# A two-layer graph network on one core: weight columns turned to rows on VectorE instead of TensorE, and the last pair of graphs done graph by graph

## The reference

```python
# layer 0: one attention weight per node, softmax over the 128 nodes of a graph
q, k = split(x @ Wqk);  v = x @ Wv
agg = adj @ (k * mask)
w = mask * sum(q * agg, axis=-1) / 16          # 128 numbers per graph
x = layernorm(x + softmax(w) * v)
# layer 1: edge weights adj * exp(q k^T), rows scaled to one
query, key, value = x @ Wq.T + bq, x @ Wk.T + bk, x @ Wv1.T + bv
weight = adj * exp(query @ key.T)
x = layernorm(x + (weight / weight.sum(-1)) @ value)
```

## Time and profile before

| | |
|---|---|
| median of 3 runs | 293.14 us (292.75 to 293.14) |
| the profiled execution | 292.77 us, of it the span of the trace 291.0 us |
| PE busy | 283.4 us, 97% of the span |
| DVE busy | 253.9 us, 87% |
| ACT busy | 238.2 us, 82% |
| POOL busy | 217.4 us, 75% |
| share of PE in the chain that ended last | 96% |
| granted clock of TensorE, mean | 0.997 |

### The profile page before, as it was taken

How to read it: one execution, slowest core, us unless ns; L and a number is a source line. 1 busy time by engine, 2 the same in 40 slices (tenths; PEclk the granted TensorE clock), 3 DMA queues, 4 the chain that set the end, 5 groups by cost and what they waited for, 6 DMA issues and landing times.

```text
span 291.0 us, 7075 instructions
## 1 busy us (share of the span) xinstructions
PE 283.4 (97%) x1984; PEld 263.7 (91%) x1984; DVE 253.9 (87%) x783; ACT 238.2 (82%) x568; POOL 217.4 (75%) x269
## 2 busy tenths in 40 slices
PE   8999999999999999999999999999999999999991
PEld 7789999999999999999999999999999999999980
DVE  1478999999989999999998999899999999999784
ACT  3455779899888989988898998889899888987862
POOL 1556987778898778789887788987787898877331
PEclk9999999999999999999999999999999999999998
DMA  7931323333334423334433333444233344210112
GB/s 241 332 97 37 91 93 127 93 91 98 106 125 126 126 93 88 99 100 126 126 124 95 88 99 100 126 126 126 94 87 96 103 126 126 90 57 26 46 38 108
DMA packets 19165, 31.26 MB, mean 107 GB/s; under 512 B 2128, under 2 KB 6608, under 8 KB 19152
## 3 DMA queue, kind: packets, MB, share of 16 engines
q1 hardware_dynamic: 19152, 31.11, 34.7%
HBM read 22.71 MB, written 8.39 MB: 107 GB/s over the span
## 4 chain that ended last, share of the span: by engine, by line
PE 96%; issue 1%; DVE 1%; POOL 0%; POOLq 0%; ACT 0%; DVEq 0%
PE ps L890 25%; PE ps L891 25%; PE ps L892 25%; PE ps L993 9%; PE ps L973 5%; PE ps L941 1%; PE ps L1112 1%; PE ps L913 1%; PE ps L1117 1%; PE ps L998 1%; PE ps L1126 1%; DVE x L661 0%; PE ps L952 0%; PE ps L960 0%; POOLq L42 0%
## 5 line engine op out<-in xcount | busy, mean ns | idle before, releaser
L890 PE MATMUL ps<-w_hi,xt_hi 128*128 128x512 f32 x124 | 49.3, 398 | 0.0
L891 PE MATMUL ps<-w_lo,xt_hi 128*128 128x512 f32 x124 | 48.6, 392 | 0.0
L892 PE MATMUL ps<-w_hi,xt_lo 128*128 128x512 f32 x124 | 48.3, 390 | 0.0
L372 POOL TENSOR_TENSOR edge_lo<-edge,edge_hi 128x256 fp32r<-128x256 f32 x29 | 21.6, 743 | 34.5 <-ACT edge_hi L544 34.5
L461 ACT ACTIVATE x<-x_sum,shift,rstd 128x256 f32<-128x256 f32 x60 | 32.8, 595 | 15.3 <-POOL shift L386 15.3
L305 POOL TENSOR_TENSOR x1b<-x,bv_all 128x512 f32<-128x512 f32 x31 | 39.7, 1282 | 2.9 <-DVE x L823 2.0
L359 POOL TENSOR_TENSOR xt_lo<-xt_raw,xt_hi 128x512 fp32r<-128x512 f32 x31 | 40.1, 1294 | 1.8 <-ACT xt_hi L443 1.8
L383 POOL TENSOR_TENSOR rstd<-var_eps,minus_half 128x4 f32<-128x4 f32 x31 | 31.6, 1018 | 9.0 <-DVE var_eps L799 9.0
L890 PE MATMUL ps<-x1t_hi,at_hi 128*128 128x256 f32 x124 | 37.4, 302 | 0.0
L366 POOL TENSOR_TENSOR x_lo<-x_raw,x_hi 128x512 fp32r<-128x512 f32 x28 | 36.2, 1294 | 0.0
L890 PE MATMUL ps<-wv_hi,x1t_hi 128*128 128x258 f32 x124 | 35.5, 286 | 0.0
(11 more groups left out here) (166 smaller groups left out, 909.5 us busy)
## 6 DMA issues: line engine op xcount, KB each, us to landing
xt_raw<-xt_pairs SPq DMA_DIRECT2D x32, 256.0 KB, 2.7
x_raw<-x_pairs SPq DMA_DIRECT2D x32, 256.0 KB, 2.7
out_pairs<-x SPq DMA_DIRECT2D x31, 256.0 KB, 2.0
adjt<-adjt_pairs SPq DMA_DIRECT2D x32, 129.0 KB, 2.1
p<-params SPq DMA_DIRECT2D x1, 770.0 KB, 6.7
p<-params SPq DMA_DIRECT2D x1, 512.0 KB, 3.8
p<-params SPq DMA_DIRECT2D x1, 256.0 KB, 4.6
out_pairs<-x SPq DMA_DIRECT2D x2, 128.0 KB, 1.8
```

What stands on the lines that cost most here:

```text
L890: nc.tensor.matmul(out, s_hi, m_hi, start=first, stop=False)
L891: nc.tensor.matmul(out, s_hi, m_lo, start=False, stop=False)
L892: return nc.tensor.matmul(out, s_lo, m_hi, start=False, stop=last)
```

## The change

Four things are done, all by other placing of small pieces of work.

First, for pairs 3 to 30 `transpose_w` leaves TensorE. VectorE turns `w_col` (now 32 columns wide, of which 30 stay zero) block by block into a new tile `w_row` in SBUF, and both the maximum and ScalarE's exponential read that tile. Second, to make place on VectorE, the bias of the scores goes to ScalarE (`bias_scores`, right behind the copy of the values); the statistics of the second layernorm are taken one slot later, behind the edges; the edges stand behind the first statistics; and `x_hi` of a pair is made earlier in ScalarE's slot. Third, `fold_biases` is cut in three, with its first part ahead of the first `transpose_w`. Fourth, the last pair's values, scores, exponentials and edges go graph by graph.

```diff
-        w_col = sb("w_col", [128, 2])
+        w_col = sb("w_col", [128, BLOCK])
+        w_row = sb("w_row", [BLOCK, NODES])
+        def w_rows(r):
+            return w_row_ps(r) if by_tensor(r) else w_row[0:2, :]
...
 ACT, slot
+                if exists(t + 3) and r + 3 >= SPLIT:
+                    split_x(t + 3, r + 3)
...
-                    nc.scalar.activation(exp_row_ps(r + 2), w_row_ps(r + 2), ACT.Exp, bias=neg_max[:, 0:1],
+                    nc.scalar.activation(exp_row_ps(r + 2), w_rows(r + 2), ACT.Exp, bias=neg_max[:, 0:1],
...
                     nc.scalar.copy(to[:, :, 0:DIM], val_ps[:, :, 0:DIM]).then_inc(val_copied, 1)
-                if exists(t + 4) and r + 4 > SPLIT:
-                    split_x(t + 4, r + 4)
+                    if r != DRAIN:
+                        bias_scores(t)
...
 DVE
+            def transpose_w(u, r):
+                for g in range(2):
+                    dve.wait_ge(w_done[g], u + 1)
+                dve.wait_ge(row_exp_done, u)
+                for b in range(0, NODES, BLOCK):
+                    block = nc.vector.transpose(w_row[:, b:b + BLOCK], w_col[b:b + BLOCK, :])
+                block.then_inc(w_row_done, 1)
...
                     for g in range(2):
                         weight(t + 2, r + 2, g)
+                    if not by_tensor(r + 2):
+                        transpose_w(t + 2, r + 2)
+                        row_max(t + 2, r + 2)
...
+                if exists(t - 2):
+                    dve.wait_ge(x2_done, t - 1)
+                    both_stats(1, x2[(r - 2) % 4]).then_inc(stats2_done, 1)
...
-                if exists(t) and r != DRAIN:
-                    bias_scores(t)
...
 PE
-                    queries(x1t_hi, x1t_lo, (t + 2, r + 2) if exists(t + 2) and r > 0 else None)
+                    queries(x1t_hi, x1t_lo, (t + 2, r + 2) if r > 0 and by_tensor(r + 2) else None)
...
             fold_scores(0)
+            fold_query_bias(0)
             transpose_w(0, 0)
...
-            fold_biases()
+            fold_query_bias(1)
+            fold_score_bias()
...
 PE, drain: values(g) now stands ahead of scores(g) for each graph; ACT: exp, then copy of val, for each graph
```

More of the change, by code:

```diff
@@ L414, in _ @@
             nc.gpsimd.memset(p_row[:, :], 0.0).then_inc(p_row_zeroed, 1)
+            nc.gpsimd.memset(w_col[:, :], 0.0)
             nc.gpsimd.memset(ident[:, :], 0.0).then_inc(ident_zeroed, 1)
@@ L472, in exp_scores, with bias_scores @@
                 last.then_inc(score_exp_done, 1)
+            def bias_scores(u):
+                act.wait_ge(score_exp_done, u)
+                nc.scalar.activation(score_bias[:, :], val_ps[:, :, DIM], ACT.Identity, bias=s_bias[:, 0:1])\
+                    .then_inc(score_bias_done, 1)
             def bias_z(to):
@@ L510, in drain @@
                 bias_z(z)
[L512 to L515, removed]
                 act.wait_ge(edge_done, b)
@@ L680, in bias_last_scores @@
             def bias_last_scores(g):
-                dve.wait_ge(last_val_done, g + 1)
+                if g == 0:
+                    dve.wait_ge(first_val_done, 1)
+                else:
+                    dve.wait_ge(val_done, PAIRS)
                 nc.vector.tensor_scalar(score_bias[:, g:g + 1], val_ps[:, g, DIM:DIM + 1], s_bias[:, 0:1], None, ALU.add)\
@@ L730, in drain @@
                 attended(a, sum_a_ps)
[L731 to L734, removed]
+                for g in range(2):
+                    bias_last_scores(g)
+                    if g == 1:
+                        dve.wait_ge(x2_done, a + 1)
+                        both_stats(1, x2[a % 4]).then_inc(stats2_done, 1)
+                    n_g = graph(g, NODES)
+                    dve.wait_ge(last_exp_done, g + 1)
+                    nc.vector.tensor_tensor(edge[:, n_g], exp_s[:, n_g], adjt[b % 4][:, n_g], ALU.mult).then_inc(last_edge_done, 1)
                 dve.wait_ge(stats2_done, a + 1)
@@ L737, in drain @@
                 variance(1)
[L739 to L742, removed]
                 dve.wait_ge(x1b_done, b + 1)
@@ L772, in slot @@
                     sum_x1(t + 1, r + 1)
+                if exists(t + 1):
+                    for g in range(2):
+                        dve.wait_ge(x1_sum_done[g], t + 2)
+                    both_stats(0, x1_sum[(r + 1) % 2]).then_inc(stats1_done, 1)
                 if exists(t - 1):
@@ L940, in transpose_w @@
                     pe.wait_ge(w_done[g], u + 1)
-                nc.tensor.transpose(w_row_ps(r), w_col[:, :], ident[:, :]).then_inc(w_row_done, 1)
+                nc.tensor.transpose(w_row_ps(r), w_col[:, 0:2], ident[:, :]).then_inc(w_row_done, 1)
             def transpose_p(u, r):
@@ L954, in fold_scores, with fold_query_bias, fold_score_bias @@
                 return mm
[L956 to L961, removed]
+            def fold_query_bias(m):
+                for k in range(HALVES):
+                    nc.tensor.matmul(bias_ps[:, m:m + 1], wq1[:, k, m * 128:(m + 1) * 128], bk[:, k:k + 1],
+                                     start=(k == 0), stop=(k == HALVES - 1))
+            def fold_score_bias():
                 pe.wait_ge(ones_ready, 1)
@@ L1042, in drain @@
                 for g in range(2):
+                    if g == 1:
+                        values(x1t_hi, x1t_lo, 1).then_inc(val_done, 1)
                     for k in range(HALVES):
```

19 lines of the change are left out of this document (7 added, 12 removed).

## The result

The changed kernel takes 294.46 us (median of 6 runs, 294.04 to 294.88) against 293.07 us before (6 runs, 292.75 to 293.27): a ratio of 1.0053, 95% interval 1.0043 to 1.0063. It is slower by 0.5%, 1.4 us, where 4 us had been forecast. The profiled execution of after took 294.88 us with a span of 292.9.

The account below looks back on a forecast made before the run. TensorE bounds the kernel before, at 8.48 us per slot; VectorE was to become the bound at 8.6. Sum: 292.77 + 5.2 (28 slots, turns included) - 0.1 - 0.4 - 0.2 = 297.3 us, stated as 297.0, range 290.5 to 300.5.

Parts of the forecast that it names:

- neg_mean: VectorE's step from neg_mean to var_eps: 0.44 us now, taken as 0.13 in the new order, so -0.31 per slot.
- attended sum: VectorE's two x2 and the maximum: 1.24 us now, less without waits for TensorE's row and its own result, -0.24 per slot.
- the new transposes wait for GpSimd: Rival: GpSimd holds VectorE's new transposes, losing up to 1.1 us per slot, 328 us; chance 0.05.
- the turn of the loop: VectorE's x_sum starts 0.32 us late in a turn's first slot; no longer hidden by slack, six times, +1.9 us.
- VectorE's slot: VectorE's time per slot from x_sum to x_sum: 8.47 us now, 8.6 us after the change, above TensorE's.
- Level: Rival: VectorE's slot is 8.43 to 8.5 us, total around 293.4 us; chance 0.12.
- TensorE's new slot: TensorE's work per slot without transpose_w, which costs about 0.11 us: 8.37 us instead of 8.48.
- TensorE remains the bound: Rival: VectorE's slot stays below 8.37 us, so all of TensorE's saved time comes back, 289.1 us; chance 0.20.
- The slack of -0.1: At the scores, 0.4 us between z's copy and TensorE's start delays the hit from VectorE's lateness; -0.1 us.
- The start: At the first transpose_w, half of the bias fold now lies in TensorE's wait for w_col; -0.4 us.
- The drain: Last pair done graph by graph, its first graph's exponential some 0.5 us earlier; -0.2 us in total.
- The second statistics only change place. 0.: VectorE's statistics of the second layernorm, taken one slot later, were to add nothing to its slot; 0 us.

Follow-up runs that it names:

- a5: The changed kernel with the four block transposes of the weights done twice, the first time into a buffer nobody reads; 318.34 us.
- a2: The changed kernel with the last-coming semaphore written first at four VectorE instructions that wait for several; 290.82 us.
- a3: The changed kernel with one of the four block transposes of the weights, the other three left out; 290.64 us.
- a1: The changed kernel with the weight columns of all pairs turned by TensorE again, all else kept; 293.15 us.
- a4: The changed kernel with the bias of the scores back on VectorE, at the end of its slot; 296.19 us.
- b2: The kernel before with the last-coming semaphore written first at three VectorE places (x_sum, first statistics, first x2); 292.53 us.
- b1: The kernel before with only the weight transposes of pairs 3 to 30 moved to VectorE, the maximum right behind them; 306.09 us.
- d1: The kernel before with the weight transposes moved to VectorE and the bias of the scores on ScalarE; 300.60 us.
- d2: The kernel before with the weight transposes on VectorE and VectorE's new order of statistics and edges, score bias still on VectorE; 296.75 us.

## Why the prediction was right and wrong

**Right: who becomes the bound.** VectorE takes over from TensorE, and the kernel gets slower. a5 shows it (+0.86 us per slot for four transposes), a2 and a3 from the other side, a1 by what the transposes cost.

**Right: most of VectorE's steps.** The steps of rows 3 to those of after: neg_mean -0.31 forecast, -0.35 measured; transposes +0.87 (0.90 less 0.03), +0.88; accumulator -0.06, -0.04; attended sum -0.24, -0.24 (0.80 and 0.20). The transpose from SBUF was priced at its neighbour's 207 ns less a little and takes 200. The Trainium skill, "VectorE: DVE Perf Modes", section on the TRN2 errata, has a table that gives 94 ns for such a block from SBUF, an estimate (58 cycles and 32 elements at 0.96 GHz), and the trace does not agree. By the fixed term of about 150 cycles that the same section calls measured it would be 190 ns, an estimate too, and the trace nearly agrees. The rival *the new transposes wait for GpSimd* fell: they run at full speed under x_lo.

**Wrong: the turn of the loop, +1.9 us.** It is 0. It had been read as a cost of the turn that slack swallows; rows 4 say only that x_sum came 0.32 us late. Records of the sequencer (in the raw trace, not in a view) show what became of it. In before the score bias at the end of the slot waits for TensorE's values, whose semaphore comes at 153.74. The bias starts at 153.77, and only then come the addition, the branch and the register move (153.78 to 154.17); the bias, 0.22 us long, is over before they are, and x_sum starts at 154.32. In after the last instructions of the slot are the transposes of p, and the same records lie under them (154.79 to 155.18, transposes 154.77 to 155.63). In a4 the bias is back, but its semaphore comes at 155.44, 0.40 us before the bias can start; the records begin at 155.48, under the transposes, and x_sum starts at 156.01, 0.17 behind the start of the bias. There the slots at the turns are 8.64 to 8.69 against 8.57 to 8.62, so 0.07 and not 0.32. Also, before has the 0.32 at five turns and not at six: behind the sixth the loop is left, and x_sum comes 0.24 behind the bias. In before these turns were not free on TensorE either (0.3 us in sum, the slots of 8.50 to 8.54); a1 and a2 have nothing of it.

**Wrong: VectorE's slot, 8.6 instead of 8.53 (238.91 / 28); 28 x 8.6 - 238.91 = 1.9 us.** One wait was missed and two gaps were. The second weight started 0.15 us behind the first one's reading in rows that the prediction didn't use (0.55 from weight to weight in before, 0.40 in after): VectorE waited there for TensorE's projection, and that goes when VectorE is late. -0.15. The bias gave back 0.05 in a typical slot (1.03 to 0.98 from the transposes of p to x_sum) instead of 0.13, since x_sum now has a gap behind the transposes (see the order of waits below); x_sum to its statistics is 0.98 instead of 0.90, for the same reason. +0.16 together. The reciprocal ahead of x2 gave 0.03 and the edges 0.03. Sum: 8.47 - 0.35 + 0.88 - 0.04 - 0.24 - 0.15 - 0.05 + 0.08 - 0.06 = 8.54, against 8.52 to 8.53 read.

Together 5.2 us forecast for 28 slots, 238.91 - 237.70 = 1.2 measured: so 4.0 us less. These two terms (1.9 and 1.9) are the error; the rest, 0.2, is that before took 237.7 in these slots and not 237.5. The total came out nearer, 294.88 us for the profiled execution against a sum of 297.3, partly by luck. It lies between the forecast and the rival *Level* (around 293.4, slots of 8.43 to 8.5). The start gave back none of its 0.4, the first slot cost 0.3 more, and in this execution all of it began 0.65 us later than in before (first transpose_w at 12.69 against 12.04; 11.68 to 12.69 over all kernels here).

**TensorE's new slot** was forecast as 8.37 and is 8.41 (a2, a3): one transpose_w on TensorE costs 0.07, not 0.11. Against a1, whose slots are 8.49 to 8.50 with the same rest of the change, it is 0.09; why a1 takes 0.02 more than most slots of before stays open. What the rival *TensorE remains the bound* would have given is therefore about 290.7 us, not 289.1, and a2 is that case: it needed 0.11 us less per slot of VectorE.

**TensorE's waits** were to be seen as 0.1 to 0.3 us per slot. They are 0.11 and can't be seen as such; z ends at 128.04 + 0.81 = 128.85 and the scores start at 128.92, so the place was right. The weight loads above show the same 0.11 (0.23 against 0.12). The slack of -0.1 is too small to find.

**The start**, -0.4: it is nothing. From the first transpose_w to the first transpose of x1 it is 12.04 to 19.03 in before and 12.69 to 19.68 in after, 6.99 us in both; it is 6.92 to 7.00 in all kernels here, with the split fold or without. The half of the fold did leave this stretch, but the next transpose_w waits for VectorE's weights, and TensorE only comes to that wait earlier (timeline of TensorE after; in before it has no such wait there):

```profile
18.61 0.27 PE L961 MATMUL ps<-ident,w_col 128*2 128x128 f32 x1 [0.49 <-DVE w_col L626]
```

Against it stands a cost that wasn't forecast: the first slot takes 7.72 to 7.74 us instead of 7.43 in every kernel here but before and b2. The timeline of VectorE after:

```profile
26.32 0.14 DVE L866 RECIPROCAL inv_sum<-exp_sum 2x1 f32<-2x1 f32 x1
26.78 0.34 DVE L871 TENSOR_SCALAR p_row<-ps,inv_sum 2x128 f32<-2x128 f32 x1 [0.32 <-DVE inv_sum L866]
```

In before the two are 0.18 apart. It stays open why: a1 has it without the transposes of w, b1 without the rest of the change.

**The drain**, -0.2: from the last transposes of x1 to the end of the span it is 14.78 us before and 14.47 after, -0.31 (14.43 to 14.59 in the kernels with the new drain, 14.72 to 14.81 in those with the old one).

**"The second statistics only change place. 0."** The sum was right and the sentence hid the largest effect of the change: without the new order, of which it is a part, the slot is 8.73 (d1), with it 8.52, and with the transposes on TensorE it is worth nothing (a1). Also neg_mean's -0.31 was taken for granted; without the bias on ScalarE and without the new order it stays (b1), and either of the two alone takes it away (d1, d2).

## What to carry to other kernels

When work moves to an engine that has nearly no room, list the loops that pass through it and its neighbours, with one sum each, and not only its own chain: here three loops lay within 0.4 us (VectorE's own 8.5, the one through the projection 8.73, and the one over ScalarE and GpSimd, 8.94 in b1), and VectorE's order of three independent instructions was worth 9 us. Waits that a bounded engine gives up when it becomes the bound (0.15 us ahead of the second weight) count against the added work; look for them between every two instructions. And where several semaphores are waited for, write the one that comes last first: 3.6 us here, but only in the kernel whose bound is that engine (b2: nothing).

## What the runs showed that had not been expected

- **The order of waits.** x_sum to its statistics is 0.97 us with the late semaphore second and 0.91 with it first, a gap of 0.10 against 0.03 us. In the instruction streams of the raw trace one wait belongs to the instruction itself and the others are instructions of their own ahead of it, with the gap where the late semaphore is among the others. As a rule it is the first one written that the instruction carries, but not always: in after x_sum carries its second one at the turn of the loop (there the step is 0.90 and not 0.98), and in a2 the first x2 carries its first one in two slots of four only (0.18 against 0.29). So look in the trace for which wait it became.
- **GpSimd and neg_mean.** In b1 neg_mean (0.16 us alone) takes 0.42 to 0.53 in the slots of the loop. In before it takes the same in most of them and 0.22 to 0.26 at the turns, in a1 and a3 0.28 to 0.43. It ends 0.01 to 0.04 us behind edge_lo each time. The Trainium skill, "SBUF — State Buffer", section on who interferes with whom, names tensor_scalar among those that can take the port shared with GpSimd; the trace agrees. In after it is not held, for VectorE comes there late enough, but only just: it takes 0.15 to 0.17 us, starts about 0.1 us before the end of edge_lo and ends 0.02 to 0.05 behind it. The new transposes (0.84 us for four under x_lo) and the statistics (0.70 to 0.72 us) are not lengthened.
- **A busy engine may wait.** TensorE shows 204.53 of 204.53 us busy in after and 204.00 of 204.00 in a2, with slots of 8.52 and 8.41. The distance between equal points of successive slots tells them apart, and at the place of the wait the weight loads do.
